# New hand-planned instruction orders on all five engines of a Mamba block plus a two-layer local-attention block

## The reference, cut to what matters

```python
# branch 1, Mamba: 512 channels, 16 states
xz = x @ in_proj_w.T; x_inner, z = split(xz)
x_conv = silu(conv4(x_inner) + conv_b)
x_dbl = x_conv @ x_proj_w.T                       # dt_lr (16), B (16), C (16)
dt = softplus(dt_lr @ dt_proj_w.T + dt_proj_b)
h_t = exp(dt_t * A) * h_(t-1) + dt_t * x_conv_t * B_t
y_t = sum_n h_t[n] * C_t[n] + x_conv_t * D
out1 = (y * silu(z)) @ out_proj_w.T
# branch 2, two layers
q, k, v = shift_token(x) @ wqkv; q, k normalised, rotary; 8 heads of 64
x = x + local_attention(q, k, v) @ wo             # windows of 128, own and previous
a, g = layernorm(shift_token(x)) @ w1 + b1
x = x + (a * gelu(g)) @ w2 + b2
```

## Time and profile before

| | |
|---|---|
| median of three runs | 2177.48 us (2172.27 to 2177.95) |
| the profiled execution, its own time | 2178.02 us |
| its span, first to last instruction | 2176.2 us |
| one steady pass (64 units), from the first scan of a chunk to that of the next | 260.0 to 263.3 us |
| PE busy (modelled) | 1946.1 us, 89% |
| DVE busy | 1905.0 us, 88% |
| ACT busy | 1648.1 us, 76% |
| POOL busy | 1044.2 us, 48% |

### The profile page before, as it was taken

One profiled execution on the slowest core, in us unless ns is written; L12 is line 12 of the kernel. 1 busy time (PEld: TensorE's weight loads), 2 busy tenths in 40 slices (PEclk: granted clock), 3 DMA queues, 4 the chain that ended last, 5 costly groups with the idle time before them and its releaser, 6 DMA issues. The chain is left out here.

```text
span 2176.2 us, 39560 instructions
## 1 busy us (share of the span) xinstructions
PE 1946.1 (89%) x11840; PEld 1318.8 (61%) x11840; DVE 1905.0 (88%) x2598; ACT 1648.1 (76%) x4031; POOL 1044.2 (48%) x1214
## 2 busy tenths in 40 slices
PE   6789899899989989899998989989899898997887
PEld 2465566666666666566665666656566665665666
DVE  3999898998989999899897999989898998997992
ACT  4776787877878878778777787877778877876672
POOL 3546454454543645445454455444454464552551
PEclk9979999999999999999999999999999999998999
DMA  5688789778887898689786898968889788887872
GB/s 184 171 207 200 185 206 225 180 174 228 197 220 184 198 228 202 170 209 237 184 210 156 207 226 195 229 177 179 213 218 231 172 181 213 195 201 180 224 166 54
DMA packets 131842, 425.22 MB, mean 195 GB/s; under 512 B 13584, under 2 KB 34832, under 8 KB 113072
## 3 DMA queue, kind: packets, MB, share of 16 engines
q0 software_dynamic: 64512, 184.58, 47.1%
q1 hardware_dynamic: 67120, 238.12, 32.4%
...
## 5 line engine op out<-in xcount | busy, mean ns | idle before, releaser
L762 DVE TENSOR_TENSOR_SCAN hb<-dA,state,hb 128x512 f32<-128x512 f32 x512 | 659.3, 1288 | 31.1 <-ACT dA L956 15.0
L1178 POOL DMA_DIRECT2D ysum<-dA x256 | 220.0, 873 | 394.7 <-DVE dA L769 295.2
L755 DVE TENSOR_TENSOR hb<-u_sb,bc 128x1024 f32<-128x1024 f32 x256 | 324.1, 1266 | 68.3 <-DMA bc<-bc_rows 62.0
L956 ACT ACTIVATE dA<-dt_sb,par 128x512 f32<-128x512 f32 x512 | 348.1, 726 | 33.9 <-DMA ysum<-dA 32.7
L1162 POOL COPY state<-hb 128x2 f32<-128x2 f32 x256 | 200.2, 784 | 334.2 <-DVE hb L762 333.6
L769 DVE TENSOR_TENSOR dA<-hb,bc 128x1024 f32<-128x1024 f32 x256 | 313.4, 1224 | 0.0
L1487 PE MATMUL ring<-hT,w 128*128 128x256 f32 x1280 | 299.4, 389 | 8.4 <-ACT hT L1104 8.4
L1058 ACT ACTIVATE rot<-rot,rnorm 128x64 f32<-128x64 f32 x1024 | 255.1, 336 | 54.4 <-DMA rot<-sq 39.2
L1487 PEld LDWEIGHTS ring<-hT,w 128*128 128x128 f32 x1280 | 243.4, 194 | 59.2 <-ACT hT L1104 20.7
L1083 ACT ACTIVATE probs<-ring,nmax 128x256 f32<-128x256 f32 x512 | 235.5, 479 | 54.3 <-DVE nmax L841 53.9
L1247 POOL TENSOR_TENSOR rnorm<-rnorm,powers 128x8 f32<-128x8 f32 x128 | 244.3, 1908 | 23.5 <-POOL rnorm L1244 21.1
...
## 6 DMA issues: line engine op xcount, KB each, us to landing
bc<-bc_rows SPq DMA_DIRECT2D x128, 1024.0 KB, 6.2
ysum<-dA POOLq DMA_DIRECT2D x256, 512.0 KB, 7.1
rot<-sq POOLq DMA_DIRECT2D x128, 256.0 KB, 4.7
...
```

The lines of the kernel that those rows point to most:

```text
L755: dve.tensor_tensor(hb[:, slot:slot + 2, :], u_pair, bc[:, g % 2, :, 0, :], ALU.mult)\
L762: dve.tensor_tensor_scan(hb[:, k % H_RING, :], dA[:, k % DA_RING, :], hb[:, k % H_RING, :], state[:, k:k + 1], ALU.mult, ALU.add).then_inc ...
L956: act.activation(dA[:, k % DA_RING, :], dt_sb[:, j, :], ACT.Exp, scale=par[:, C_ALOG + n:C_ALOG + n + 1]).then_inc(dA_ready.sem, 1)
L1178: pool.dma_start(ysum[j, :, :], dA[:, out:out + 2, :].rearrange("p n t -> p (n t)"), accum_op=ALU.bypass if first else ALU.add).then_inc(a ...
```

## The change: new order tables

Nothing is computed otherwise. All fifteen order strings are replaced (`PE`, `DVE`, `ACT`, `POOL`, `SP`, each as `_FIRST`, `_ORDER` and `_LAST`); each holds the same steps in another sequence. Every instruction that was there is still there, and the same number of times. One line of the steady list of SP as an example:

```diff
 SP_ORDER = """
-+v(1) +v(2) +bc(1) y(1) +bc(2) +bc(3) xres(1) +q(1) +q(2) +w1(0) +bc(4) store(0) store(1) +k(1) +wol(0)
-+k(2) ++x(0) ++x(1) +w2(0) +bc(5) +bc(6) +bc(7) +v(3) +v(4) +k(3) +k(4) +q(3) +bc(8) +bc(9) +bc(10) +bc(11)
-+bc(12) +bc(13) +xres(0) +w1(1) +wol(1) +k(5) +k(6) +w2(1) ++xdbl +q(4) +q(5) +bc(14) +q(6) +q(7) ++q(0)
++q(1) +q(2) +v(1) +bc(1) y(1) +bc(2) +bc(3) xres(1) +wol(0) store(0) +bc(4) +bc(5) +w1(0) store(1) +w2(0)
+++x(0) +k(1) +bc(6) +v(2) +bc(7) +k(2) +k(3) +v(3) +v(4) ++x(1) +bc(8) +q(3) +bc(9) +bc(10) +bc(11) +k(4)
++q(4) +k(5) +q(5) +q(6) +xres(0) +bc(12) +w1(1) +w2(1) +wol(1) +k(6) +bc(13) +y(0) +bc(14) +bc(15) +q(7)
```

More of the change, by code:

```diff
@@ L88 @@
++s(6,1) +h(2,0) +h(2,1) +h(2,2) +h(2,3) +h(2,4) +h(2,5) +pT(6,0) +pT(6,1) +rb(6) +pT(6,2) +pT(6,3) +v(7)
++o(6,0) +o(6,1) +w2(2) +o(6,2)
 """
 DVE_ORDER = """
[L90 to L102, removed]
++scan +scan w2(2) +scan o(6) +turn(q,0) m(7,0) m(7,1) +turn(k,0) m(7,2) m(7,3) +scan rinv(7) +scan +scan
+o(7) wo(6) wo(7) stats(3) +scan +scan +m(0,0) +m(0,1) +turn(q,1) +m(0,2) +m(0,3) +scan gate(1) +scan h(3,0)
@@ new lines @@
++turn(k,1) +scan branch(0) h(3,1) h(3,2) +scan h(3,3) h(3,4) h(3,5) +scan +scan w2(3) +scan +scan +rinv(0)
+branch(1) +scan +scan +turn(q,2) +turn(k,2) +scan +m(1,0) +m(1,1) +scan +m(1,2) +m(1,3) +scan +scan +rinv(1)
++o(0) +scan +scan +u(1) ++norm(0) +wo(0) +o(1) +scan +turn(q,3) +wo(1) +m(2,0) +m(2,1) +m(2,2) +m(2,3)
++stats(0) +scan +turn(k,3) +scan +rinv(2) +scan +scan +h(0,0) +h(0,1) +scan +h(0,2) +h(0,3) ++norm(1) +scan
++h(0,4) +h(0,5) +scan +scan +scan +m(3,0) +m(3,1) +m(3,2) +m(3,3) +o(2) +w2(0) +scan +scan +rinv(3) +scan
@@ L103 @@
++gate(0) +h(2,4) +h(2,5) +scan +scan
 """
 ACT_ORDER = """
[L105 to L109, removed]
@@ L122 @@
++rb(5) +turn(q,6) +turn(k,6) +dA +v(6) +heads(6) +q(7) +dA +hn(2) +k(7) +hT(2) +e(6,0) +e(6,1) +dA +dA
++e(6,2) +e(6,3) +dA +h(2,0) +h(2,1) +last(2) +h(2,2) +h(2,3) +h(2,4) +h(2,5) +pT(6,0) +dA +pT(6,1)
++turn(q,7) +turn(k,7) ++dA +rb(6) +pT(6,2) +pT(6,3) ++skip(0) ++dA
 """
 POOL_ORDER = """
[L124 to L125 removed]
@@ L126 @@
[L126 to L130, removed]
@@ new lines @@
++q(3) +scan +scan +add(9) +add(10) ++norm(0) +scan +turn(q,3) +rot(q,3) +stats(0) +add(11) +rot(k,3) +scan
++scan +add(12) +turn(k,3) +add(13) +carry ++norm(1) +scan +add(14) +scan +scan +q(4) +add(15) +add(16)
++add(17) +scan +rot(q,4) +rot(k,4) +turn(q,4) +scan +skip(1) +turn(k,4) +stats(1) +scan +add(18) +add(19)
++q(5) +scan +rot(q,5) +rot(k,5) +add(20) +q(6) +scan +turn(q,5) +turn(k,5) +add(21) +scan +add(22) +merge(0)
++scan ++tail +add(23) +scan +add(24) +add(25) +scan +rot(q,6) +rot(k,6) +turn(q,6) +scan +turn(k,6) +add(26)
@@ new lines @@
+rinv(0) scan scan turn(q,2) turn(k,2) scan scan scan o(0) scan scan m(1,0) m(1,1) m(1,2) m(1,3) u(1) scan
+scan rinv(1) +norm(0) scan scan turn(q,3) turn(k,3) scan o(1) scan scan m(2,0) m(2,1) m(2,2) m(2,3) wo(0)
+wo(1) scan scan stats(0) scan scan scan +norm(1) scan scan scan scan h(0,0) h(0,1) h(0,2) scan h(0,3) h(0,4)
+h(0,5) rinv(2) scan scan m(3,0) m(3,1) m(3,2) m(3,3) scan scan scan scan w2(0) scan rinv(3) o(2) scan scan
+scan turn(q,4) turn(k,4) o(3) scan scan wo(2) wo(3) scan stats(1) scan scan scan turn(q,5) turn(k,5) scan
@@ L165 @@
+scan scan h(1,0) h(1,1) h(1,2) h(1,3) h(1,4) h(1,5) m(4,0) m(4,1) m(4,2) m(4,3) scan scan w2(1) scan scan
+scan rinv(4) turn(q,6) turn(k,6) m(5,0) m(5,1) scan m(5,2) m(5,3) scan o(4) scan scan rinv(5) scan o(5) scan
+wo(4) wo(5) m(6,0) m(6,1) m(6,2) m(6,3) stats(2) scan scan scan rinv(6) turn(q,7) turn(k,7) scan h(2,0)
+h(2,1) scan h(2,2) h(2,3) +u(0) h(2,4) h(2,5) scan gate(0)
 """
 ACT_FIRST = """
-xn(0) xnT(0) xn(1) q(0) xnT(1) in(0) start(0) k(0) in(1) in(2) in(3) turn(q,0) silu(0) silu(1) turn(k,0)
@@ L181 @@
+e(6,2) e(6,3) dA pT(6,0) hn(2) v(6) q(7) hT(2) last(2) k(7) pT(6,1) dA dA dA h(2,0) h(2,1) h(2,2) pT(6,2)
+h(2,3) h(2,4) h(2,5) rb(6) +dA pT(6,3) turn(q,7) turn(k,7) +skip(0) +dA
 """
 POOL_FIRST = """
-norm(0) halo q(0) norm(1) rot(q,0) rot(k,0) q(1) turn(q,0) turn(k,0) turn(q,1) turn(k,1) tail rot(q,1) q(2)
-rot(k,1) scan scan add(0) add(1) +halo turn(q,2) turn(k,2) rot(q,2) rot(k,2) skip(0) q(3) scan scan add(2)
-add(3) scan scan add(4) add(5) turn(q,3) add(6) scan q(4) add(7) scan +norm(0) rot(q,3) rot(k,3) scan add(8)
@@ L191 @@
-turn(k,7)
+q(0) norm(0) halo norm(1) rot(q,0) rot(k,0) q(1) turn(q,0) turn(k,0) turn(q,1) rot(q,1) rot(k,1) scan
+turn(k,1) add(0) q(2) add(1) rot(q,2) scan scan rot(k,2) skip(0) scan q(3) turn(q,2) turn(k,2) add(2) scan
+add(3) scan add(4) add(5) scan turn(q,3) turn(k,3) rot(q,3) rot(k,3) +norm(0) add(6) add(7) scan q(4) scan
+add(8) scan stats(0) add(9) tail +halo scan +norm(1) scan add(10) scan carry add(11) add(12) add(13) scan
+scan scan add(14) add(15) scan scan add(16) add(17) rot(q,4) rot(k,4) scan turn(q,4) skip(1) turn(k,4) q(5)
@@ L231 @@
++rinv(5) +scan +wo(4) +scan +scan +scan +o(5) +turn(q,7) +turn(k,7) +wo(5) +m(6,0) +m(6,1) +m(6,2) +m(6,3)
++stats(2) +scan +scan +scan +scan +h(2,0) +scan +scan +rinv(6) +h(2,1) +h(2,2) +h(2,3) +h(2,4) +h(2,5) +scan
++scan +w2(2) +m(7,0) +m(7,1) +m(7,2) +m(7,3) +rinv(7) +o(6) +o(7) +wo(6) +wo(7) +stats(3) +gate(0) +gate(1)
++h(3,0) +h(3,1) +h(3,2) +h(3,3) +h(3,4) +h(3,5) +branch(0) +w2(3) +branch(1)
 """
 ACT_LAST = """
-heads(7) +dA v(7) +q(0) +k(0) e(7,0) e(7,1) pT(7,0) pT(7,1) e(7,2) e(7,3) +dA +dA pT(7,2) +dA +dA pT(7,3)
```

255 lines of the change are left out of this document (124 added, 131 removed).

## The result

The changed kernel takes 2234.27 us (median of 4 runs, 2229.7 to 2240.8), the kernel before in the same job 2175.73: a ratio of 1.0273, 95% interval 1.0241 to 1.0304. The forecast was 2155, a gain of 1.0%, with a range that ended at 2200. It is a loss of 2.7%, some 59 us.

A forecast was written before the change was run, and what follows sets the result against it. It took DVE and PE as the bound, with 22 to 25 us idle per steady pass. Terms summed to -3.6 us a pass, -22 for six; with last pass -4 and first +3, 2178.0 became 2155 us, range 2115 to 2200.

The forecast's parts named there:

- Steps 1, 3 and 5: DVE's waits per steady pass for bc(5), for bc(14) and at turn(q,3) go: -6.5, -3.5 and -2.3 us.
- Step 2: Weights now stand ahead of bc(6), so DVE waits at scan #24: +3.5 us a steady pass (0 to 8.1).
- Step 4: Weights and a table now stand ahead of bc(13), so DVE waits for it: +4.1 us a pass (0.2 to 8.7).
- The rate of the queue: SP's queue in a burst moves 173 KB/us, with 149 and 200 as the ends, taken from three bursts.
- A: Rival: SP's queue keeps up at 200 KB/us or more, so both new bc waits vanish; 2110 us, chance 0.14.
- Step 6: Two small DVE waits per steady pass shrink: m(7,0) gets a turn ahead, -1.0 us; the kept state, -0.8.
- Steps 7 and 8: New DVE waits per steady pass: bare hand-overs at the end of block 7, +1.0 us; Gelu output h(3,0), +1.9.
- estimate of 206 KB/us: Queue rate scaled from 173 KB/us by the HBM limit; both new bc waits would vanish, giving the time of A.
- B: Rival: weights block bc(6) and bc(13) longer than they had blocked bc(5) and bc(14); 2211 us, chance 0.28.
- C: Rival: no change, idle time is given back at hand-overs between DVE, PE and ACT; 2178 us, chance 0.18.
- First pass: w2(0) ahead of bc(0) and y(0) behind bc(0), which delays gate(0): +3 us (-3 to +6).
- Last pass: The store start(0) waits for loses w2 and the table ahead of it: -4 us (0 to -9.6).

The follow-up runs named there:

- Runs 6: Kernel before the change, with only the load bc(5) moved ahead of k(2), x(0), x(1) and w2(0) on SP's steady list: 2138.94 us, ratio 0.9834.
- run 7: Kernel before the change, bc(5) moved early and bc(13) put behind xres(0), w1(1), wol(1), ahead of k(5), k(6), w2(1), on SP's steady list: 2104.08 us.
- run 1: Changed kernel, rotary table load k(1) moved directly behind bc(5), ahead of the weights, on SP's steady list: 2195.71 us, 1.0078 of the kernel before.
- run 4: Changed kernel with k(1) behind bc(5), w2(1), wol(1) and k(6) behind bc(13), and x(1) behind bc(7): 2123.50 us, 0.9737 of the kernel before.
- run 5: Changed kernel, SP's lists unchanged, q(3) on POOL's steady list moved behind two scan steps and add(9): 2194.57 us, 1.0083 of the kernel before.
- run 3: Changed kernel, token load x(1) moved directly behind bc(7), ahead of k(2), k(3), v(3), v(4), on SP's steady list: 2204.93 us, 1.0111 of the kernel before.

## Why the prediction was wrong, step by step

- **Steps 1, 3 and 5** (no wait for `bc(5)`, none for `bc(14)`, none of 2.3 at `turn(q,3)`) held. Runs 6 and 7 price the first two on their own: 7.1 us a pass for `bc(5)`, 4.8 for `bc(14)` (254.7 to 249.9), where the waits were 6.5 and 3.5.
- **Step 2** (`bc(6)`, +3.5) measured 0 in the changed kernel, though its two halves were nearly right. The batch from `bc(5)` to the table, 3968 KB from 902.5 to 925.2, ran at 175 KB/us, where I took 173. But `bc(6)` itself landed 9.6 us after its issue at 918.0, so all 4992 KB took 25.1 us and not 28.9, at 199 KB/us. And it could not show anyhow: DVE already stood for POOL until 926.3. With that stall away, runs 1 and 4 show only 0.7 us in one pass: there `bc(6)` landed 23.9 to 27.3 us after the issue of `bc(5)`, and DVE wanted it after 26.6 to 26.8, where I had 25.4. In run 5 the wait is 0.5 to 1.3 in five of six passes.
- **Step 4** (`bc(13)`, +4.1) was right in place and low in size: 5.5 to 7.6 in six passes, and 9.1 with what followed it. In the pass shown both of its terms were off: the 4992 KB took 30.2 us and not 28.9 (165 KB/us; 159 to 169 in the six passes), and DVE wanted the rows 23.8 us after the issue of `bc(12)` and not 24.8. SP stood at `w2(1)` until PE had used the old one, from 1023.9 to 1032.1, but its queue did not run dry for it, since `w1(1)` landed at 1032.0. What went slowly was the second part: 896+512+128+1024 KB in the 20.3 us from there, 126 KB/us (151 if the 512 KB of `y(0)` from 1041.7 on are counted in). The DMA engines were busy all the time, at 1.02 of their share, but by the packets of each queue POOL's had 0.59 of it and SP's 0.42:

```profile
1032.08:1052.38 20.30, 19.39 (x132) 11.11 (x130) 13.52 (x15) 19.47 (x53) 4.88 (x7) 1.00 1.02 266
```

- **The rate of the queue** rested in part on a misread burst. The 162 KB/us of the earlier trace rows leave out `bc(13)`, issued 0.4 us ahead of the batch, at 1537.0, and landed at 1541.9. With its 1024 KB, 4352 KB went in 20.9 us, 208 KB/us, and 204 to 214 in the six passes before the change. So two of the three bursts had reached 200, their mean is 186 and not 170, and the argument against A, that both bursts of a steady pass gave 149 and 162, was only half true. One rate for both new waits was the wrong picture too, since it went by what POOL's queue took in each (last section).
- **Step 6**: `m(7,0)` waits no more, and the 0.8 us for the kept state at scan #42 went; but that wait came back as 5.6 to 6.6 at scan #22.
- **Steps 7 and 8** came out at about +2.3 (`wo(7)` 2.2 and `stats(3)` 1.4, against 1.2 before) and +0.6, together 2.9 as in my sum: the total is right, the split is not.
- **The step that failed** is the sentence after the sum: "Everything else I cost at nothing. POOL is idle half of the time and its lists keep the transfers near the scans that feed them". The table load had been in my batch of step 2, as 128 of its 4992 KB, but I followed only the last load of the batch to its user. POOL wanted the table 11.65 us before it landed, and DVE stood for the copy behind it on POOL's list. The tokens `++x(1)`, which moved from ahead of `bc(5)` to behind `v(4)`, cost 3.4 us of DVE a pass. Neither is a term of the sum. The first is worth 38.6 us (run 1), the second 29.3 (run 3). With these prices the sum of -22 would have come out at about +46 for the steady passes, which is what the profile has (+46.8), though part of that agreement is luck, since step 2 was too high and step 4 too low.
- **The rivals.** A (the queue keeps up) is out for `bc(13)` and was true for `bc(6)`. The batches of `bc(6)` moved 199 to 207 KB/us in the six passes, those of `bc(13)` 159 to 169. The 301 GB/s that I took as full is not the most: the engines moved 315 from 1022.2 to 1032.1, and 266 in the row above at the same share of 1.02. The estimate of 206 KB/us, from the limit in the Trainium skill (DMA: Bandwidth & Descriptors, Specifications), was nearly met by the batches of `bc(6)` and missed by those of `bc(13)`; the limit itself, about 358 GB/s, was reached in none of these stretches. B gave a loss, of 33 us, but not for the reason that the runs show. It wanted more than 11 us in the two new `bc` waits; they came to 5.5 to 7.6, less than the 10.0 of the old ones, and the loss came from loads that B had not in it. C, the hand-overs, fell with run 4; with run 7 beside it, the new hand-overs cost the steady passes no more than the old ones.
- **First pass**: forecast +3, measured +3.2; no run takes it apart, so the number can be luck.
- **Last pass**: forecast -4, measured +4.2. The store did come 1.3 us earlier for ACT, but `bc(12)` behind `y(0)`, `xres(0)`, `wol(1)` and `w1(1)` was not looked at: 8.1 us at scan #48.
